# A side buffer for the middle piece of the last block in layers 2 and 3, another order of layer 2's finish, and fewer edge-table units ahead of the first sort's turns

## The reference

```python
def _L2_gnn_ref(node_emb, edge_emb, W1_msg, b1_msg, W2_msg, b2_msg, W1_upd, b1_upd, W2_upd, b2_upd, senders, receivers):
    msg_in = jnp.concatenate([edge_emb, node_emb[senders], node_emb[receivers]], axis=-1)
    h = jax.nn.silu(msg_in @ W1_msg + b1_msg)
    edge_messages = h @ W2_msg + b2_msg
    node_messages = _segment_mean(edge_messages, receivers, node_emb.shape[0])
    upd_in = jnp.concatenate([node_emb, node_messages], axis=-1)
    hu = jax.nn.silu(upd_in @ W1_upd + b1_upd)
    return hu @ W2_upd + b2_upd

def _L3_gnn_ref(h, edge_index, adj_v, deg_v, W, b, deg_coeff, coeff_param, scale_param):
    Wh = h @ W + b
    row, col = (edge_index[0], edge_index[1])
    # cosine similarity of Wh[row] and Wh[col], split by its sign, weights Wh[col] in a sum over row
    ...
    return scale * (coeff[0] * prop_pos + coeff[1] * prop_neg + coeff[2] * Wh)
```

## Time and profile before

| | |
|---|---|
| median of 3 runs | 3170.77 us (3169.61 to 3173.38) |
| profiled execution | 3168.21 us, its span 3166.4 us |
| POOL busy | 2202.2 us, 70% of the span |
| VectorE (DVE) busy | 1318.1 us, 42% |
| TensorE (PE) busy, weight loads (PEld) | 643.9 us, 477.8 us |
| ScalarE (ACT) busy | 496.7 us, 16% |
| mean granted TensorE clock | 0.576 of full speed |

### The profile page before, as it was taken

How to read it: one execution, slowest core, us unless ns; L and a number is a source line. 1 busy time by engine, 2 the same in 40 slices (tenths; PEclk the granted TensorE clock), 3 DMA queues, 4 the chain that set the end, 5 groups by cost and what they waited for, 6 DMA issues and landing times. The chain is left out here.

```text
span 3166.4 us, 14581 instructions
## 1 busy us (share of the span) xinstructions
PE 643.9 (20%) x3384; PEld 477.8 (15%) x3385; DVE 1318.1 (42%) x1864; ACT 496.7 (16%) x463; POOL 2202.2 (70%) x2299
## 2 busy tenths in 40 slices
PE   5421130002410000001888850001000600000001
PEld 5411110001300000001567630000000400000001
DVE  8888875102210000008466642242435405353455
ACT  2200007111100000001100122232323211221220
POOL 0177777777677777777777767777776367777774
PEclk8765565555555555555899975555555555555555
DMA  9211124212355766654355424333332132323231
GB/s 330 97 25 14 14 27 110 51 33 64 78 50 54 62 61 59 64 56 58 80 136 150 111 51 81 98 108 108 92 124 80 21 63 72 89 72 90 72 90 48
DMA packets 195122, 248.82 MB, mean 79 GB/s; under 512 B 138380, under 2 KB 149229, under 8 KB 187510
## 3 DMA queue, kind: packets, MB, share of 16 engines
q0 software_dynamic: 74048, 114.24, 19.7%
q1 hardware_dynamic: 62950, 104.45, 10.3%
q10 hardware_dynamic: 58064, 29.51, 8.2%
HBM read 154.12 MB, written 93.93 MB: 78 GB/s over the span
## 5 line engine op out<-in xcount | busy, mean ns | idle before, releaser
L808 POOL DMA_INDIRECT l0g_rows<-in_rec_s,ents x440 | 427.8, 972 | 138.5 <-issue 133.8
L763 POOL DMA_INDIRECT l1g_rows<-tab,srct x440 | 416.2, 946 | 144.5 <-issue 133.8
L763 POOL DMA_INDIRECT l2g_rows<-tab,ep_rows x440 | 416.1, 946 | 134.1 <-issue 134.1
L763 POOL DMA_INDIRECT l3g_rows<-tab,others x440 | 415.2, 944 | 134.1 <-issue 134.1
L1268 POOL DMA_INDIRECT ep_rows<-recp,entd x352 | 348.9, 991 | 107.3 <-issue 107.3
L1465 DVE TENSOR_TENSOR l1s_A<-l1s_A,l1s_mk 110x4096 f32<-110x4096 f32 x1 | 4.4, 4422 | 539.9 <-ACT l1s_A L1442 539.9
L1720 PE MATMUL l1a_pa<-l1a_g,l1a_wt 128*128 x1296 | 168.8, 290 | 0.0
L1720 PEld LDWEIGHTS l1a_pa<-l1a_g,l1a_wt 128*128 128x128 f32 x1296 | 158.3, 202 | 24.1 <-issue 24.1
L2250 DVE COPY l2g_mix<-l2g_q 128x64 f32<-128x64 f32 x12 | 2.7, 228 | 318.2 <-ACT l2g_mix L2221 318.2
L2596 DVE COPY l3g_filled<-l3g_q 128x65 f32<-128x65 f32 x12 | 2.7, 228 | 310.9 <-ACT l3g_filled L2565 310.9
L2657 PE MATMUL l3t_nmp<-ident,l3t_nmb 128*64 128x128 f32 x2 | 0.7, 448 | 583.6 <-DVEq L2674 583.6
(11 more groups left out here) (566 smaller groups left out, 2446.8 us busy)
## 6 DMA issues: line engine op xcount, KB each, us to landing
l1a_g<-g SPq DMA_DIRECT2D x54, 390.0 KB
recp<-ep_rows ACTq DMA_DIRECT2D x11, 1320.0 KB, 5.7
g<-l1g_rows ACTq DMA_DIRECT2D x10, 1430.0 KB, 25.3
sums<-l0s_sums SPq DMA_DIRECT2D x10, 1408.0 KB
sums<-l2o_sums SPq DMA_DIRECT2D x9, 1408.0 KB
sums<-l3o_sums SPq DMA_DIRECT2D x9, 1408.0 KB, 5.4
rowsd<-ep_rows POOLq DMA_DIRECT2D x8, 1452.0 KB, 5.8
ep_rows<-rowsd SPq DMA_DIRECT2D x8, 1452.0 KB, 6.6
```

What stands on the lines that cost most here:

```text
L763: nc.gpsimd.indirect_dma_start(out=ring.rows[:, s, j, :], out_offset=None, in_=table, in_offset=bass.IndirectOffsetOnAxis(ap=index(b, s, j ...
L808: nc.gpsimd.indirect_dma_start(out=rows[:, j, :], out_offset=None, in_=K.a["rec_s"], in_offset=bass.IndirectOffsetOnAxis(ap=K.by_src.ent[: ...
```

## The change

`SIDE` is part 10, the middle piece. In both gathers it gets a buffer of its own (in layer 2 in the two banks that the product of the nodes has left, in layer 3 in the last two banks, where the weight moves in behind `filled`). ScalarE turns part 10 ahead of the pack of part 9, and part 11 ahead of the pack of part 10. In layer 2's finish the carries have two banks of their own and are computed in four steps, two of them inside the loop, and VectorE finishes group t-3, in the place between averaging group t and joining group t-1. `AHEAD` goes from 20 to 15. Cut to its core:

```diff
...
@@ -60,6 +60,8 @@
 LAST = ((0, 24), (24, 12), (36, 8))
 GROUPS = [(w, min(4, NT - w)) for w in range(0, NT, 4)]
 NG = len(GROUPS)
+SIDE = NBLK
+CARRY_AT = (2, 4)
 
 
 class Kern:
@@ -562,7 +564,7 @@
             engine.wait_ge(self.stored[s], len(range(s, NEB, STAGES)) * 16)
 
 
-AHEAD = 20
+AHEAD = 15
 
 
 def units_after(m):
...
         mix_banks = ph.ps("mix", (P, 6 * 512))
-        turn, own = ph.ps("turn"), ph.ps("own")
+        pair = ph.ps("pair", (P, 2 * 512))
+        turn, own = pair[:, 0:512], pair[:, 512:]
         share = T.own[D:, :]
         at = ph.sb("at", [D, 4 * P])
         shared, turned, moved, projected = ph.sems("shared", "turned", "moved", "projected")
...
 
+        def bank_of(i):
+            return pair if i == SIDE else mix_banks
...
 
+                def turn_rows(i):
+                    b, c0, n, landed, count = parts[i]
+                    act.wait_ge(landed, count)
+                    if i == SIDE:
+                        act.wait_ge(moved, 2 * NG)
+                    elif i > SIDE:
+                        act.wait_ge(packed, SIDE)
+                    elif i:
+                        act.wait_ge(packed, i)
+                    nc.scalar.copy(cut(bank_of(i), n)[:, :, 1:],
+                                   ring.rows[:, b % RING, c0:c0 + n, D:].rearrange("p j f -> p f j")).then_inc(spread, 1)
+
                 act.wait_ge(blank, 1)
                 mask(keeps, K.by_dst.keep, 0, kept)
                 for i, (b, c0, n, landed, count) in enumerate(parts):
-                    s = b % RING
-                    mix = cut(mix_banks, n)
-                    act.wait_ge(landed, count)
-                    if i:
-                        act.wait_ge(packed, i)
-                    nc.scalar.copy(mix[:, :, 1:], ring.rows[:, s, c0:c0 + n, D:].rearrange("p j f -> p f j")).then_inc(spread, 1)
+                    mix = cut(bank_of(i), n)
+                    if i < SIDE:
+                        turn_rows(i)
                     mask(afters, K.by_dst.after, i, trailed)
                     act.wait_ge(mixed, i + 1)
                     nc.scalar.activation(mix[:, :, 1:], mix[:, :, 1:], ACT.Silu).then_inc(acted, 1)
                     if i + 1 < len(parts):
                         mask(keeps, K.by_dst.keep, i + 1, kept)
+                    if SIDE <= i + 1 < len(parts):
+                        turn_rows(i + 1)
                     act.wait_ge(scanned, i + 1)
...
         K.tab3_stored = (stored, 2 * NG * 16)
-        carry_banks = (pa[0], pa[1], pb[0], pb[1])
+        carry_banks = [ph.ps(f"carried{i}") for i in range(2)]
         wh = K.wh
...
                 pe.wait_ge(made, 3)
-                for w in range(NT):
-                    lt = nc.tensor.matmul(carry_banks[w // 8][:, w % 8 * D:(w % 8 + 1) * D], sel[:, w * P:(w + 1) * P], car[:, :],
-                                          start=True, stop=True)
-                    if w % 8 == 7 or w == NT - 1:
-                        lt.then_inc(carry, 1)
-                pe.wait_ge(kept, 4)
+
+                def carries(i):
+                    if i >= 2:
+                        pe.wait_ge(kept, i - 1)
+                    for w in range(8 * i, min(8 * i + 8, NT)):
+                        lt = nc.tensor.matmul(carry_banks[i % 2][:, w % 8 * D:(w % 8 + 1) * D], sel[:, w * P:(w + 1) * P], car[:, :],
+                                              start=True, stop=True)
+                    lt.then_inc(carry, 1)
+
+                carries(0)
+                carries(1)
                 for t in range(NG + 2):
+                    if t in CARRY_AT:
+                        carries(2 + CARRY_AT.index(t))
                     if t < NG:
                         w, n = GROUPS[t]
                         pe.wait_ge(averaged, t + 1)
...
             def _(act):
-                for i, bank in enumerate(carry_banks):
+                def keep_carries(i):
                     w, n = 8 * i, min(8, NT - 8 * i)
                     act.wait_ge(carry, i + 1)
-                    nc.scalar.copy(carried[:, w:w + n, :], bank[:, 0:n * D].rearrange("p (w d) -> p w d", d=D)).then_inc(kept, 1)
+                    nc.scalar.copy(carried[:, w:w + n, :],
+                                   carry_banks[i % 2][:, 0:n * D].rearrange("p (w d) -> p w d", d=D)).then_inc(kept, 1)
+
+                keep_carries(0)
+                keep_carries(1)
                 for t in range(NG + 1):
+                    if t in CARRY_AT:
+                        keep_carries(2 + CARRY_AT.index(t))
                     if t < NG:
                         n = GROUPS[t][1]
                         act.wait_ge(turned, t + 1)
...
                 wide = lambda c, ws, n: c[:, ws].unsqueeze(2).to_broadcast([P, n, D])
-                for t in range(NG + 2):
+                for t in range(NG + 3):
                     if t < NG:
                         w, n = GROUPS[t]
                         ws = slice(w, w + n)
...
                         v.tensor_tensor(res[:, ws, :], res[:, ws, :], wide(T.r, ws, n), ALU.mult).then_inc(averaged, 1)
-                    if 1 <= t <= NG:
-                        u = t - 1
-                        w, n = GROUPS[u]
-                        dve.wait_ge(first, u + 1)
-                        if u >= 2:
-                            dve.wait_ge(acted, u - 1)
-                        v.tensor_tensor(both[:, u % 2, 0:n * P], pb[u % 2][0:D, 0:n * P], T.own[0:D, w * P:(w + n) * P], ALU.add).then_inc(joined, 1)
-                    if t >= 2:
-                        u = t - 2
+                    if t >= 3:
+                        u = t - 3
                         w, n = GROUPS[u]
                         ws = slice(w, w + n)
                         dve.wait_ge(second, u + 1)
@@ -2469,6 +2492,13 @@
                         v.tensor_tensor(sq[:, ws, :], K.hn[:, ws, :], K.hn[:, ws, :], ALU.mult)
                         v.drain()
                         v.tensor_reduce(var[:, ws], sq[:, ws, :], AX.X, ALU.add)
+                    if 1 <= t <= NG:
+                        u = t - 1
+                        w, n = GROUPS[u]
+                        dve.wait_ge(first, u + 1)
+                        if u >= 2:
+                            dve.wait_ge(acted, u - 1)
+                        v.tensor_tensor(both[:, u % 2, 0:n * P], pb[u % 2][0:D, 0:n * P], T.own[0:D, w * P:(w + n) * P], ALU.add).then_inc(joined, 1)
                 v.drain()
                 v.tensor_scalar(var[:, :], var[:, :], 1.0 / D, 1e-5, ALU.mult, ALU.add)
                 v.drain().then_inc(spread, 1)
...
         neg = ph.sb("neg", [P, TB])
-        filled = ph.ps("filled", (P, 6 * 512))
-        weight = ph.ps("weight")
+        banks = ph.ps("banks", (P, 8 * 512))
+        filled, beside = banks[:, 0:C1 * FLAT], banks[:, 6 * 512:]
+        weight = banks[:, C1 * FLAT:C1 * FLAT + TB]
         blank, got, spread, masked, scanned, packed, cut_masked = ph.sems(
             "blank", "got", "spread", "masked", "scanned", "packed", "cut_masked")
...
 
+                def turn_rows(i):
+                    b, c0, n, landed, count = parts[i]
+                    act.wait_ge(landed, count)
+                    if i > SIDE:
+                        act.wait_ge(packed, SIDE)
+                    elif i and i != SIDE:
+                        act.wait_ge(packed, i)
+                    nc.scalar.copy(cut(bank_of(i), C1, n)[:, :, 1:],
+                                   ring.rows[:, b % RING, c0:c0 + n, C1:].rearrange("p j f -> p f j")).then_inc(spread, 1)
+
                 act.wait_ge(blank, 1)
                 mask(keeps, 0, masked)
                 for i, (b, c0, n, landed, count) in enumerate(parts):
-                    s = b % RING
-                    act.wait_ge(landed, count)
-                    if i:
-                        act.wait_ge(packed, i)
-                    nc.scalar.copy(cut(filled, C1, n)[:, :, 1:], ring.rows[:, s, c0:c0 + n, C1:].rearrange("p j f -> p f j")).then_inc(spread, 1)
+                    if i < SIDE:
+                        turn_rows(i)
...
                     act.wait_ge(scanned, i + 1)
                     if b and c0 == 0:
                         act.wait_ge(stored, i * 16)
-                    nc.scalar.copy(sums[:, c0:c0 + n, :], by_entry(cut(filled, C1, n)[:, 0:D, 1:])).then_inc(packed, 1)
...
```

More of the change, by code:

```diff
@@ L2246, in _ @@
                     s = b % RING
-                    mix, size = cut(mix_banks, n), D * (n + 1)
+                    mix, size = cut(bank_of(i), n), D * (n + 1)
                     dve.wait_ge(spread, i + 1)
@@ L2530, in cut, with bank_of @@
             return t[:, 0:f * (n + 1)].rearrange("p (f j) -> p f j", f=f)
+        def bank_of(i):
+            return beside if i == SIDE else filled
         with Step(nc, pool_ahead=True) as block:
@@ L2568, in _ @@
                         act.wait_ge(stored, i * 16)
-                    nc.scalar.copy(sums[:, c0:c0 + n, :], by_entry(cut(filled, C1, n)[:, 0:D, 1:])).then_inc(packed, 1)
```

(3 more changed lines are left out.)

## The result

The changed kernel takes 3143.63 us (median of 4 runs, 3141.52 to 3151.84), the kernel before takes 3170.19 us beside it (4 runs, 3168.59 to 3173.38): a ratio of 0.992, 95% interval 0.9899 to 0.994. Forecast were 3144.3 us in a range of 3134 to 3154. The profiled execution of the changed kernel is the longest of its four, 3151.84 us with a span of 3150.0 us; so its own distance to the trace of before, 16.4 us of span, understates the change. The same kernel was profiled again later (run a0_again, span 3141.1 us), and so was the kernel before (run b0_before, 3164.7 us).

What follows compares the result with a forecast made beforehand. POOL's fixed-pace gathers were taken to bound the kernel, with time to win only where POOL waits; 5.7 + 3.0 + 5.1 + 12.7 = 26.5 us off gave 3141.7 us, 3144.3 on the median's footing, range 3134 to 3154.

Steps and rivals of the forecast that it cites:

- layer 2's finish: Layer 2's finish: split carries and VectorE's new order leave TensorE's 4.85 us a group as the longer; gain 12.7 us.
- first gather earlier: First sort: 15 units ahead instead of 20 cut VectorE's 7.20 us wait at its first turn; gain 5.7 us.
- layer 2's drain: End of layer 2's gather: part 10 turned early into its own buffer, part 11 starting after its rows land; gain 3.0 us.
- layer 3's drain: End of layer 3's gather: the same edit removes VectorE's waits before parts 10 and 11; gain 5.1 us.
- So it fits, with 0.4 us left: First sort, later turns: one more unit costs 0.89 us against ScalarE's 1.28 us of slack.
- the slower rival: First sort: six turns wait some 14 us each for the edge table's stores, total 3228 us; chance 0.03.
- The averages' small slack: Layer 2's finish: the averages arrive with 0.2 us to spare, and a slip costs only itself.
- the early start alone buys only the transpose of group 0: Layer 2's finish: starting transposes before all 25 carry windows are done wins only group 0's transpose.
- the rival of the old pace: Layer 2's finish: joins come late each time, only the first transpose's 3 us are won, total 3154 us; chance 0.10.
- The clock rival: Layer 2's finish: TensorE's clock rises above 1.2 GHz, about 6 us more gained, some 3135 us; chance 0.13.
- the sort gains: Rival for the first sort: it gains nothing, as the first turn waits for saturated DMAs, total 3150.0 us; chance 0.08.
- the edits are hidden: Whole kernel: POOL waits elsewhere, so the time does not change; chance 0.02.

Runs made afterwards that it cites:

- k2: The changed kernel with five units after odd turns to m = 9 and VectorE's old order in layer 2's finish, carries still split; 3153.34 us, one run.
- a0_third: The changed kernel, nothing edited, on the slower kind of chip; 3963.44 us, ratio 0.9948 to the kernel before.

## Why the prediction was right

The total came out 0.7 us from the forecast, and that it came so close is luck: the sort gave 3 to 5 us less than its term, the finish more, and the same kernel gained 26.6 us in the one comparison and 28.4 in the other. Step by step:

| step | forecast | after | a0_again |
|---|---|---|---|
| first gather earlier | 5.7 (3 to 6.6) | 0.8 | 2.4 |
| layer 2's drain | 3.0 (2.3 to 3.1) | 3.0 | 3.1 |
| layer 2's finish | 12.7 (8 to 19) | 13.9 | 16.2 |
| layer 3's drain | 5.1 (4.5 to 5.3) | 5.0 | 4.9 |
| sum | 26.5 | 22.7 | 26.6 |

(Differences of the first gather's start and of GpSimd's waits to the trace of before. Up to the variance step the finish is 14.0 us shorter in after and 14.1 in a0_again; the rest of the 16.2 is above all the landing of the last store of layer 3's table, 5.1 us for 6.8. The spans shrank by 16.4 and 25.3 us; what they are short of the sums lies in the gathers between these places, which the change doesn't touch. The second trace of the kernel before has 61.2 us for the finish's wait where the first has 63.2, so this row is uncertain by some 2 us; up to the variance step both have 65.3.)

**The first sort** is the step that failed, and it lies below its own lower bound. The wait at the first turn went as written, 7.20 to 0.88. "So it fits, with 0.4 us left", said of one more unit, held for all turns but one. The one it missed is the unit behind m = 5 that opens block 6 and needs block 4's store. It is the fifth of six there; a sixth unit after a turn opens a block only behind m = 3. "That store has 10 to 13 us by my schedule", says the prediction: it had 11.7 in the first trace (75.97, where ScalarE began to wait, less 64.23) and 10.2 in a0_again (75.58 less 65.39), but it took 16.3 and 13.8. This is the mechanism of the slower rival, which I had at "over about 18 us, six times". It acts as soon as the store outlasts those 10 to 12 us, and it acted once: VectorE lost 3.7 and 2.2 us. And that the last store "comes up to 0.9 us closer to the store of the sorted keys, which is inside what I took off" was wrong: it came 1.50 us closer (0.19 for 1.69; 0.01 in a0_again), and VectorE's wait behind the keys' store grew by 1.5 and 1.3 us. With five units a turn to m = 9 (k2) both are gone, and the first gather is 7.6 us earlier than before, more than I had allowed. That "what is won at each reaches the end of the program" isn't shown for the sort: in k2 5.1 of these 7.6 us were left at layer 2's first gather.

**The drains** came as worked out, the landing included: 3.63 us from the last issue to part 11 against 3.58. The moved weights and ScalarE's writes beside VectorE's scans cost nothing that shows.

**The finish.** The round was forecast at TensorE's 4.85 us and is 4.79; the variance step, forecast 52.6 us behind the first gather (2505.8 less 2453.25), comes at 51.3: the last group's first product ends 44.7 us behind the first gather for 45.3 in the sum (2498.5 less 2453.25), and what VectorE does behind it takes 6.6 for 7.3. The averages' small slack held. That "the early start alone buys only the transpose of group 0" gave it too much, as did the 3 us that the rival of the old pace kept: k2 has the split carries with the old order and gains nothing.

**The clock rival** fell: 24.00 us without a pause stayed at 1.2 GHz. The Trainium skill, "TensorE: Matmul & The Clock Gate", section "What's actually happening", has sustained activity release the throttle. By that the window should have been at 2.4 GHz; this case's windows don't agree, in the kernel before and in this one. What did raise the clock in layer 1 no run here shows.

**The other rivals**: the loop doesn't keep its old pace, and the sort gains, so both are out as cases, though the sort's came near: its gain of 0.8 us in the profiled run is closer to none than to 5.7. That the edits are hidden is out by the ratio, 0.992 with an interval that ends at 0.994.

**Two slips in its sums** changed nothing: the lower bounds of the four terms add up to 17.8 us and the upper ones, with the finish at its 12.7, to 27.7, where it has 16 and 27, and a sixth unit follows five turns, where the sort's lower bound counts six.

## What to carry to other kernels

When work is spread differently around the points where another engine waits, follow each unit with its buffer: one unit more is cheap until it is the one that opens a buffer whose store is still under way, and then the wait lasts until that store has landed. A round of three engines can be set by the order in which the engine between serves finished and unfinished groups; here that order alone was worth 14 us, and an early start ahead of it nothing. Where a large store has no haste, keep it away from the small one that somebody waits for.

## What the runs showed of the hardware that I had not expected

The store of the sorted keys (SyncE's queue) is waited for longer the closer ahead of it the table's store of 1320 KB (ScalarE's queue) is issued. Distance between the two issues, and VectorE's wait: 4.34 us, 3.25; 2.55, 3.25; 1.70 (b0_before), 3.91; 1.69, 3.92; 0.76, 4.86; 0.55, 5.07; 0.19, 5.43; 0.01, 5.22. In a0_third the table's store is issued 0.33 us after the keys' store, and the wait is 3.25 again. So a store shortly ahead goes with up to 2.2 us more, and at 2.55 us nothing of it is seen. These are the traces of different kernels, not one parameter varied alone, and the 3.25 us at 4.34 and at -0.33 are of the slower kind of chip, on which no store close ahead was seen.

A 1320 KB store of the edge table takes 4.5 to 4.6 us when no other transfer of size is beside it. Issued between 64 and 71 us, while the 800 KB stores of layer 0's table are under way, it takes 10.5 to 16.3 us in the seven traces of the first kind of chip, and 16.3 and 13.8 us in the two of the changed kernel there.

Chips differ: the kernel before takes 3167 to 3170 us on some and 3985 to 3988 us on others, with the same instructions. The same change is worth 26.6 and 28.4 us on the one kind and 21.6 on the other, where GpSimd stands 345 us for a table and 184 us for VectorE.
